# A two-layer decoder on one core: three moves in the third stage, and a fifth stage whose bias is added by TensorE, in a new order

## The reference

```
# block 2: a gated memory (mLSTM) over ctx, 8 heads of 16
log_D  = where(tril, csum_i - csum_j, -inf) + input_gate_j
D      = exp(log_D - max(log_D))
C      = (q k^T / 4 + q . rpe[hops]) * D
h      = (C / (max(|sum(C)|, exp(-max)) + 1e-6)) @ v
hn     = (h - mean_head(h)) / sqrt(var_head(h) + 1e-5) * (1 + ln_w) + ln_b
# block 3: causal attention with rope, 16 heads of 8, then top-2 of 8 experts
# block 4: x = layernorm(x + causal attention with rope, 16 heads of 8)
# block 5: cross attention of x over ctx, 16 heads of 8
scores = (x Wq + bq) * 8**-0.5 . (ctx Wk + bk) + attn_bias + attention_mask
x      = layernorm(x + softmax(scores) @ (ctx Wv + bv) @ Wo + bo)
# block 6: top-2 of 16 experts
```

## Time and profile before

| what | value |
|---|---|
| median of 3 runs | 4294.4 us (4290.12 to 4306.48) |
| the profiled execution | 4309.58 us, span of its core 4307.5 us |
| mean granted PE clock | 0.811 |
| PE busy | 2919.2 us, 68% |
| DVE busy | 2641.8 us, 61% |
| POOL busy | 1897.7 us, 44% |
| ACT busy | 1600.9 us, 37% |
| PE's clock in 40 equal slices of the span | `9999999967888887875589978888888775588855` |

### The profile page before, as it was taken

One profiled execution on the slowest core, in us unless ns is written; L12 is line 12 of the kernel. 1 busy time (PEld: TensorE's weight loads), 2 busy tenths in 40 slices (PEclk: granted clock), 3 DMA queues, 4 the chain that ended last, 5 costly groups with the idle time before them and its releaser, 6 DMA issues.

```text
span 4307.5 us, 91934 instructions
## 1 busy us (share of the span) xinstructions
PE 2919.2 (68%) x27246; PEld 1985.7 (46%) x27249; DVE 2641.8 (61%) x7148; ACT 1600.9 (37%) x3994; POOL 1897.7 (44%) x2306
## 2 busy tenths in 40 slices
PE   4999998768777777872068878888888770066610
PEld 2666665335444454541046555555555550055510
DVE  2777776447778777874011178888888873044455
ACT  2666665324444444431023244444444440011100
POOL 4222222035565555653720065555555534711167
PEclk9999999967888887875589978888888775588855
DMA  2111111521111111111222110000000001211133
GB/s 52 39 41 38 42 38 37 196 80 40 43 45 38 45 39 39 43 29 37 74 73 75 58 29 24 25 23 26 26 23 24 23 18 45 71 54 54 54 80 87
DMA packets 282376, 207.13 MB, mean 48 GB/s; under 512 B 61730, under 2 KB 246455, under 8 KB 281904
## 3 DMA queue, kind: packets, MB, share of 16 engines
q1 hardware_dynamic: 262960, 164.88, 13.1%
q0 software_dynamic: 19200, 39.62, 3.4%
HBM read 114.99 MB, written 90.18 MB: 48 GB/s over the span
## 4 chain that ended last, share of the span: by engine, by line
PE 20%; DVE 15%; issue 14%; POOL 5%; DVEq 1%; DMA 0%; ACT 0%; POOLq 0%; ACTq 0%
PE scores_ps L1038 3%; PE scores_ps L893 3%; DVE z L1848 2%; POOL rows L2047 2%; DVE row_max L1556 2%; PE scores_ps L902 2%; POOL shared L2144 2%; PE heads_ps L1087 1%; PE scores_ps L1148 1%; PE desk_ps L1045 1%; PE heads_ps L1045 1%; PE turned_ps L908 1%; DVE norm_stat L1534 1%; PE scores_ps L1150 1%; DVE row_max L1837 1%
## 5 line engine op out<-in xcount | busy, mean ns | idle before, releaser
L1991 POOL TENSOR_TENSOR norm_rstd<-norm_veps,minus_half 128x1 f32<-128x1 f32 x384 | 241.2, 628 | 500.7 <-DVE norm_veps L1538 499.8
L1259 ACT ACTIVATE probs<-probs 128x512 f32<-128x512 f32 x384 | 240.6, 627 | 231.3 <-DVE probs L1558 217.7
L2047 POOL DMA_INDIRECT rows<-e_in,slot_put x256 | 249.0, 973 | 163.9 <-issue 107.4
L902 PE MATMUL scores_ps<-consts,probs 128*128 128x128 f32 x1536 | 293.5, 333 | 9.8 <-ACT probs L1259 9.0
L1263 ACT ACTIVATE turned<-scores_ps 128x512 f32<-128x512 f32 x384 | 226.1, 597 | 79.9 <-PE scores_ps L902 70.0
L902 PEld LDWEIGHTS scores_ps<-consts,probs 128*128 128x128 f32 x1536 | 218.2, 172 | 74.4 <-ACT probs L1259 62.5
L1475 DVE TENSOR_REDUCE row_max<-scores_ps 128x8 f32<-128x512 f32 x256 | 174.8, 683 | 63.0 <-PE scores_ps L756 58.1
L1191 ACT ACTIVATE probs<-probs 128x512 f32<-128x512 f32 x256 | 161.4, 630 | 136.3 <-DVE probs L1477 133.9
L1900 DVE COPY shared<-turned_ps 128x256 f32<-128x256 f32 x72 | 30.5, 424 | 266.1 <-PE turned_ps L1140 266.1
L1556 DVE TENSOR_REDUCE row_max<-scores_ps 128x8 f32<-128x512 f32 x256 | 174.3, 681 | 14.6 <-issue 10.1
L1558 DVE TENSOR_TENSOR probs<-scores_ps,row_max 128x512 f32<-128x512 f32 x256 | 177.0, 691 | 8.8
(11 more groups left out here) (338 smaller groups left out, 8772.8 us busy)
## 6 DMA issues: line engine op xcount, KB each, us to landing
hop_dram<-shared SPq DMA_DIRECT2D x64, 256.0 KB, 2.1
hop_in<-hop_dram SPq DMA_DIRECT2D x64, 256.0 KB
rows<-zero_rows SPq DMA_DIRECT2D x64, 144.0 KB, 1.9
shared<-rows SPq DMA_DIRECT2D x72, 128.0 KB, 2.1
moe<-shared SPq DMA_DIRECT2D x72, 128.0 KB, 1.9
rows<-zero_rows SPq DMA_DIRECT2D x64, 128.0 KB, 1.8
c_in<-in_ctx SPq DMA_DIRECT2D x128, 64.0 KB, 2.3
c_two<-in_ctx SPq DMA_DIRECT2D x128, 64.0 KB
```

The lines of the kernel that those rows point to most:

```text
L902: last = pe.transpose(scores_ps[:, a, g, P * k:P * k + P], probs[a][:, P * hp:P * hp + P], ident)
L1259: act.activation(half, half, ACT.Exp, scale=scale).then_inc(at.exped.sem, 1)
L1991: pool.tensor_tensor(n_rstd[:, k, u, :], n_veps[:, k, u, :], minus_half[:, 0:1], ALU.pow).then_inc(sig.sem, 1)
L2047: pool.indirect_dma_start(out=rows, out_offset=bass.IndirectOffsetOnAxis(ap=slot_put[:, c, U * n + i:U * n + i + 1], axis=0), in_=put_rows ...
```

## The change

Third stage: on ACT the square stands ahead of the values' copy. On POOL the spread of the memory keys waits also for the last apply of the tile before (`mixed.of(i - 1)`). On DVE the `f_norm` apply stands ahead of the first apply of `mixed`. On PE the memory scores move from the start of the next period to the place ahead of the transpose of `xn`.

Fifth stage: the bias of attention b goes into its scores on PE: `bias5` multiplies `fm` by the f32 identity into both banks ahead of the scores, as the causal mask does for a. `bias_and_shift5` goes, and b uses `shift5` (4 counts instead of 6). The steps of all five engines stand in a new order: attention b now scores tile i instead of i - 2, and x6 is stored for tile i - 2 instead of i - 4.

More of the change, by code:

```diff
@@ L929, in period @@
                 u, j4 = j % U, j % 4
[L930 to L939, removed]
                 if live(i - 1):
@@ L1004, in period @@
                     last.then_inc(m_weighed.sem, 1)
+                if live(i + 2):
+                    after(pe, (zeroed, U + 1), m_spread.of(i + 2), m_shift.of(i + 1, 4), m_copied.of(i + 1))
+                    keys = k_ring[u][:, 0:MH // NR * P].rearrange("p (h t) -> p h t", t=P)
+                    for g in range(NR):
+                        rows = slice(64 * g, 64 * g + 64)
+                        for b in range(NB):
+                            last = pe.matmul(scores_ps[S * b:S * b + S, 0, g, 0:256],
+                                             xT_ring[(j + 2) % 8][rows, S * b:S * b + S], keys[rows, :, S * b:S * b + S],
+                                             start=True, stop=True, skip_group_check=True)
+                    last.then_inc(m_scored.sem, 1)
                 if live(i):
@@ L1065, in period @@
                 if live(i - 1):
[L1066 to L1069, removed]
+                    turn_ctx5(a5[1], 1, i - 1)
+                if live(i + 1):
+                    turn5(a5[0], 0, i + 1, 1)
                 if live(i - 2):
-                    after(pe, (zeroed, U + 1), b_q_copied.of(i - 2), b_spread.of(i - 2), a5[1].copied.of(i - 3))
-                    scores5(a5[1], 1, b_q[u], k_ring[2 + u], False)
@@ L1076, in period @@
                 if live(i - 1):
[L1077 to L1089, removed]
@@ new lines, in period @@
+                    causal5(0)
+                if live(i + 1):
+                    turn_ctx5(a5[0], 0, i + 1)
+                if live(i + 2):
+                    after(pe, (zeroed, U + 1), a_spread.of(i + 2))
+                    scores5(a5[0], 0, q_ring[:, u, :], k_ring[u])
+                if live(i + 1):
+                    project5(0, i + 1, l_w[:, 5, :])
+                if live(i + 3):
+                    after(pe, x4_copied.of(i + 3))
+                    for k in range(4):
+                        last = pe.matmul(heads_ps[:, P * k:P * k + P], l_w[:, k, :], x_T[1 - u], start=True, stop=True,
+                                         skip_group_check=True)
+                    last.then_inc(a_roped.sem, 1)
@@ L1406, in period @@
                     exp5(a5[0], 0, i + 1, 1, SCALE)
+                    copy5(a5[0], 0, i + 1, 0)
+                if live(i - 1):
+                    after(act, a5[1].ctx_turned.of(i - 1))
+                    act.activation(o_T[1], heads_of[1][:, 384:512], ACT.Identity, bias=c_col[:, 3:4])\
+                       .then_inc(o_copied[1].sem, 1)
+                if live(i + 1):
+                    copy5(a5[0], 0, i + 1, 1)
+                if live(i - 2):
+                    after(act, x6_turned.of(i - 2), c_turned.of(i + 1))
+                    act.activation(x6_T[u], desk_ps[:, 0:P], ACT.Identity).then_inc(x6_copied.sem, 1)
@@ new lines, in period @@
+                if live(i + 1):
+                    after(act, b_keys.of(i + 1), b_spread.of(i - 1))
+                    act.activation(b_k[1 - u], desk_ps[:, P:2 * P], ACT.Identity, bias=c_col[:, 1:2])\
+                       .then_inc(b_k_copied.sem, 1)
+                if live(i):
+                    copy5(a5[1], 1, i, 0)
+                if live(i + 1):
+                    after(act, a5[0].ctx_turned.of(i + 1))
+                    act.activation(o_T[0], heads_of[0][:, 384:512], ACT.Identity).then_inc(o_copied[0].sem, 1)
```

291 lines of the change are left out of this document (136 added, 155 removed).

## The result

The new kernel took 4123.4 us in the median (4115.7 to 4126.2, four runs) beside 4300.4 for the kernel before (4290.1 to 4318.4): a ratio of 0.9576, interval 0.9551 to 0.9600, so 177 us less where 155 were forecast from the profiled run, and 4123 where the forecast was 4140. By the ratio it is 182 us less. The profiled execution took 4115.7 us, its span 4113.5, against 4309.6 and 4307.5.

What follows compares the result with a forecast made beforehand. The prediction took stages 3 and 5 to be bound by hand-offs between engines, with part of PE's work at half clock. Stage 3 -61, stage 5 -86, fill and drain -8 sum to -155 us: 4140 us, range 4035 to 4240.

Steps and rivals of the forecast that it cites:

- the path over POOL in stage 5: Stage 5: from DVE's first shift half through POOL's powers, gathers and key spread to DVE's last apply, 14.35 us per tile.
- (a): Stage 3, ACT's square ahead of the values' copy: h_var waits for nothing, -1.28 us on DVE; at 1.2 GHz mostly a gm wait.
- (b): Stage 3, POOL's spread held until xn is done: -0.7 us per tile on DVE.
- (c): Stage 3, f_norm apply ahead of the other: fills a wait for one rstd, lengthens the next; gain nothing.
- (d): Stage 3, memory scores move into PE's wait for xn; roped starts 0.45 us earlier, h_T's copy exposed, some 0.45 us idle.
- -8 for filling and draining: Stage 5: cross attention follows two periods sooner, so filling and draining take two half-empty periods less: -8 us (0 to -20).
- in a third of the periods that adds 0.6: Stage 5: PE slow from the x4 transpose on lengthens a third of the periods, bringing 14.35 to 14.9 us.
- Rival A: Clock up: stage 5 takes 14.35 us per tile, stage 3 DVE's 14.5; 4040 us in all; chance 0.17.
- The combine's meeting with the spread: Stage 5: the combine's second step (L1848) no longer meets POOL's spread in the new order, -1.47 us per tile.
- Rival B: PE takes what DVE gives: stage 5 stays at 16.3 us per tile, stage 3 alone gains; 4237 us; chance 0.21.
- Rival C: Slower: bias products delay PE's queue in stage 5, clock stays 0.81, period 18.4 us; 4371 us; chance 0.06.
- Rival D: Nothing: new waits eat the gains in both stages, 4294 +- 20 us; chance 0.06.

Runs made afterwards that it cites:

- s5_only: The new kernel with the four moves of stage 3 undone: 4176.4 us, ratio 0.9701 to the kernel before.
- get_early: The new kernel with POOL's index copy and two gathers of stage 5 issued ahead of the power for x4: 4082.4 us, ratio 0.9493.
- bias_old_order: The kernel before with only the bias product on PE in place of DVE's addition, in stage 5's old order: 4340.9 us, ratio 1.0111.
- undo_spread: The new kernel with POOL's spreads in stage 3 no longer held until the last apply: 4143.6 us, ratio 0.9624.
- bias_both: The new kernel with b's bias added on DVE again and PE's bias products kept but overwritten by the scores: 4203.5 us, ratio 0.9787.
- gm_first: The new kernel with the decay mask's product issued ahead of the out product on PE in stage 3: 4075.8 us, ratio 0.9488.
- undo_scores: The new kernel with the memory scores back behind the norm's transpose on PE in stage 3: 4079.9 us, ratio 0.9468.

## Why the prediction came out as it did

**The number holds, and so does the path over POOL in stage 5; the clock's term there was too large, and stage 3's number came right by luck.** The sum gave -155, the medians -177 (the profiled runs -194, since that of before was a long one and that of after a short one).

*Stage 3, 15.5 us and -61.* Measured 15.47, and -64 or -65. By steps: (a) the square is off DVE's path; about half of its 82.0 us turned into waits for PE, as forecast in kind: 31.3 for 17.3 us at L936, 23.3 for 4.5 at L954, 10.4 for 0.3 at L949. (b) the spread held, xn at 346 ns, holds. (c) the f_norm apply moved, put at nothing: no run undoes it, but the rows show the exchange that was forecast, DVE's wait for r_tmp's power down from 25.6 to 9.4 us and that for xn's up from 18.1 to 34.8. (d) is where the argument failed. It read PE's wait for xn, 0.9 us, as something for the scores to fill, and subtracted it in full, though with (a) and (b) in place and the scores left behind the transpose only 0.2 us per tile of it is left. The two errors cancel in the sum: the wait does go, but moving the scores costs 0.68 us per tile instead of saving some. That 15.5 met 15.47 is therefore luck. A sum for PE with the other moves already in it would have spoken for leaving the scores where they were (14.79 measured). It would still have missed the clock, 0.84 with the move and 0.89 without, in which that difference stands. The three losses undone singly (+18, +21, -46) don't add to the 65 either: which of square and spread counts depends on what else is there. Both undone at once was not tried. The causal product issued ahead of the spread's wait stood in no term; 15.70 without it and 15.35 to 15.59 with it is little more than the noise, and `s5_only`, with it and the old stage 3, has 16.39 for 16.46.

*Stage 5, 14.9 us and -86, and -8 for filling and draining.* Measured 14.15 in the middle of the stage, 14.00 over all, and -125 for the stage with its drain. The -86 took 16.24 us for all 64 tiles, but before the change the mean over them was 15.75: while the pipeline fills, the first combines follow one another faster, ten periods in 130.8 us, and the new kernel takes 131.5 for these. So the periods gave 1.75 x 63 = 110 us, not the 2.09 x 64 of the middle. Filling gave nothing. The other 15 us are the drain: 71.2 us from the last combine to the last sum of the logits before, 56.6 now. By its steps, in the period shown: DVE from its first shift half to the end of the statistics of b_sum, where POOL's power starts, 7.30 (7.4 forecast), power 0.51, index copy and gathers 3.29 (3.2), spread 1.85 (1.9), power and wait 0.62, the apply 0.39 from start to start (0.70): 13.96 in all. The forecast's 14.35 is a slip, for its own terms make 14.3. `get_early` shows that this was the path. **The step that was mis-sized is the clock's: "in a third of the periods that adds 0.6".** The clock rose from 0.81 to 0.98, and nothing was added. The bias product cost what was forecast: its four passes with PE's next product start 1.78 us apart, for 1.75.

```profile
2628.23 1.94 PE L888 MATMUL scores_ps<-fm,consts 128*128 128x512 f32 x4
2630.01 0.38 PE L1077 MATMUL desk_ps<-h_T,c_w 128*128 128x128 f32 x2
```

DVE's own work, put at 11.7 us, comes to 10.8 from the forecast's own terms (13.6 - 1.4 - 1.47); 11.1 was measured (550.98 us in 700, a tile every 14.15). For PE's 13.3 no working is shown; that `get_early` has a period of 13.37 fits it. Rival A had the clock of stage 5 right (0.98) and that of stage 3 wrong (0.84).

*The combine's meeting with the spread* is gone as forecast (352 ns). *Rival B* (PE takes what DVE gives) failed because PE's waits shrank with DVE's chain. *Rival C* failed in the new order; the same mechanism, with no new order to go with it, is what `bias_old_order` shows, 48 us slower. *Rival D* failed.

*The lock.* 346 against 1050 ns for xn, with nothing changed but POOL's wait (`undo_spread`), shows the meeting as the cause. These rows agree with the lock of the Trainium skill, "SBUF — State Buffer", section "Who interferes with whom". Its rule spoke against the new last apply of stage 5: the meeting does cost there, 462 ns for 337 in `get_early`, where the apply meets nothing.

## What to carry to other kernels

Where two engines wait for each other in turn, make the sum for each with all the other moves in it: a wait that one edit has shortened holds less of what another moves into it. Take back each part of a change that came out well: one of its four moves in stage 3 cost 46 us. When a period changes, split an engine's share of it into idle and busy time before naming the cause: twice here the idle time per tile stayed or grew, and the same products took less time at a higher clock. In an order written out by hand look for long instructions that stand ahead of a short one for which another engine waits (the gathers ahead of the power, the out product ahead of the mask's), and move the long one to a place where its engine stands waiting anyway.

## What the runs showed that was not expected

A higher granted clock need not give time. In `bias_old_order` it rose from 0.81 to 0.90 and the kernel lost 48 us; in `bias_both` from 0.89 to 0.94 with the period the same within noise. The clock rose as well with no product added and no idle time taken away: `gm_first` and `undo_scores` have PE's products of the new kernel in another order, idle 3.43 and 3.11 us per tile for 3.16, and 0.91 and 0.89 for 0.84 in stage 3. There the period fell with it.
